# Local attention's first tiles: tables and norms ahead of the last band operations, third rows turned sooner, the output weights' split later

## The reference

```python
x = x + _L0_xattn_ref(_layernorm(x), ctx_1024, ctx_1024, mask)      # band attention, |i - j| <= 128
x = x + _L0_ffn_ref(_layernorm(x), wqkv, ...)                       # two layers of:

h = shift_token(x)                      # second half of the channels from the row before
q, k, v = split(h @ wqkv)               # 8 heads of 64
q = l2norm(q) * q_scale;  k = l2norm(k) * k_scale
q, k = rotary_xpos(q, k)                # q * cos * scale + rotate_half(q) * sin * scale
o = local_attention(q, k, v)            # keys i-256 .. i
x = x + o @ wo
h = layernorm(shift_token(x)) * lg + lb
a, g = split(h @ w1 + b1)
x = x + (a * gelu(g)) @ w2 + b2
```

## Time and profile before

| | us |
|---|---|
| median of 3 runs | 3015.71 (3015.14 to 3015.97) |
| the profiled execution | 3016.03 |
| its span in the profile | 3014.1 |
| PE busy | 2972.0 (99%) |
| DVE / ACT / POOL busy | 1610.6 / 1239.6 / 1135.9 (53%, 41%, 38%) |
| granted PE clock, mean | 0.996 |

### The profile page before, as it was taken

The page is one execution under the profiler, slowest core; times in us unless marked ns, Lnnn a source line. Parts: engine busy times, 40 slices in busy tenths (PEclk is TensorE's granted clock), DMA queues, the critical chain, the costliest instruction groups (busy, mean ns, idle before and its releaser), DMA issues. The chain is left out here.

```text
span 3014.1 us, 44257 instructions
## 1 busy us (share of the span) xinstructions
PE 2972.0 (99%) x17040; PEld 2420.4 (80%) x17040; DVE 1610.6 (53%) x3359; ACT 1239.6 (41%) x2497; POOL 1135.9 (38%) x1200
## 2 busy tenths in 40 slices
PE   8999999999999999999999999999999999999999
PEld 6787888888878888888887788888878888888887
DVE  6975667766765333333324766776675333433331
ACT  6874555555664111111114555555565212111111
POOL 6755556556641101111103555655661111211111
PEclk9999999999999999999999999999999999999999
DMA  7542111111132111001122111111114111111110
GB/s 246 198 162 78 43 39 50 57 43 43 40 104 74 45 45 45 31 20 39 45 78 75 33 43 50 47 50 43 54 57 133 57 45 31 53 55 52 46 53 29
DMA packets 144181, 190.52 MB, mean 63 GB/s; under 512 B 21334, under 2 KB 75098, under 8 KB 143972
## 3 DMA queue, kind: packets, MB, share of 16 engines
q1 hardware_dynamic: 143972, 187.70, 19.6%
HBM read 132.44 MB, written 52.46 MB: 61 GB/s over the span
## 5 line engine op out<-in xcount | busy, mean ns | idle before, releaser
L991 PE MATMUL quad<-fhT_f,w_h_f 128*128 128x512 f32 (+1 forms) x1392 | 551.0, 396 | 1.5 <-ACT w_h_f L1055 1.5
L993 PE MATMUL quad<-fhT_f,w_l_f 128*128 128x512 f32 (+1 forms) x1392 | 545.0, 391 | 0.0
L992 PE MATMUL quad<-fhT_f,w_h_f 128*128 128x512 f32 (+1 forms) x1392 | 543.4, 390 | 0.0
L1650 DVE SCALAR_TENSOR_TENSOR u_f<-quad,bias_f,gate_f_raw 128x512 f32<-128x512 f32 (+1 forms) x174 | 130.4, 750 | 699.0 <-PE quad L993 616.3
L1719 POOL TENSOR_SCALAR stats<-stats 128x1 f32<-128x1 f32 x64 | 43.5, 679 | 1020.2 <-DVE stats L1625 1019.5
L1805 POOL TENSOR_TENSOR turned_qk<-with_cos,with_sin 128x256 f32<-128x256 f32 x256 | 188.8, 759 | 452.4 <-DVE with_cos L1534 361.0
L1210 ACT ACTIVATE lprob<-lprob,small 128x384 f32<-128x384 f32 (+2 forms) x512 | 289.8, 568 | 160.4 <-DVE small L1509 160.4
L1313 ACT ACTIVATE gate_f_raw<-quad,bias_f 128x512 f32<-128x512 f32 (+1 forms) x174 | 119.8, 689 | 506.7 <-PE quad L993 506.7
L1055 ACT ACTIVATE uT_f<-u_f 128x512 fp32r<-128x512 f32 (+2 forms) x176 | 117.5, 668 | 510.9 <-DVE u_f L1650 510.9
L761 PE MATMUL bank_pair<-wqkv_h,hT 128*128 128x512 f32 x992 | 319.8, 403 | 1.1 <-DVE with_sin L1534 1.1
L993 PEld LDWEIGHTS quad<-fhT_f,w_l_f 128*128 128x128 f32 (+1 forms) x1392 | 256.8, 184 | 63.1
(11 more groups left out here) (221 smaller groups left out, 6039.1 us busy)
## 6 DMA issues: line engine op xcount, KB each, us to landing
s_in<-stream SPq DMA_DIRECT2D x128, 128.0 KB, 2.7
s_res<-stream SPq DMA_DIRECT2D x64, 256.0 KB, 2.9
stream<-a_out SPq DMA_DIRECT2D x64, 256.0 KB, 2.0
w_h_f_raw<-in_L_ffn_w SPq DMA_DIRECT2D x60, 256.0 KB, 5.3
h_in_f<-stream SPq DMA_DIRECT2D x112, 128.0 KB, 2.5
res_f<-stream SPq DMA_DIRECT2D x47, 256.0 KB, 3.2
x_in<-in_x SPq DMA_DIRECT2D x32, 256.0 KB, 2.8
ctx_in<-in_ctx SPq DMA_DIRECT2D x32, 256.0 KB, 3.1
```

The lines of the kernel that those rows point to most:

```text
L991: e.matmul(bank[0:n, :], high, hT[:, 0, c, :], start=c == 0, stop=False)
L992: e.matmul(bank[0:n, :], high, hT[:, 1, c, :], start=False, stop=False)
L993: ins = e.matmul(bank[0:n, :], low, hT[:, 0, c, :], start=False, stop=c == KC - 1)
L1650: e.scalar_tensor_tensor(out=Fm.u[q % 2][0:n, :], in0=up_bank(2 * (g * HC + j) + 1)[0:n, :], scalar=Fm.bias1[0:n, 0, j:j + 1], in1=Fm.gate ...
```

## The change

In `band()`, step 36: ACT gets `square(0, 0)`, DVE `norm_sum(0, 0)` ahead of the last `band_add_x`, POOL `scale_tables(0)` and `inverse_norm(0, 0)` ahead of the last `band_offset(.., "x1")`. In `attend` of layer 1, DVE's `norm_sum` of tile 0 stands ahead of its ropes and POOL's `inverse_norm` ahead of its rotation. The key half of tile 0's rotation goes from POOL to DVE (`rotate_first_keys`), with a semaphore of its own. PE turns rows 2 after 12 of tile 1's 24 q and k products, and the order of the turns of q and k and tile 1's v products is new. DVE takes `split_h(s + 1)` ahead of the divisions where the attended tile starts a batch entry. `wo` is split one step later, and an Exp on a small tile is placed in ACT's step 0 of layer 1. Functions that `band()` now calls too move out of `attend`.

```diff
@@ tensor_program, attend
                 if s == 1:
-                    project(l, 1, 12, 36)
+                    project(l, 1, 12, 24)
                     turn_h(2)
+                    project(l, 1, 24, 36)
+                    turn_q(0)
                     project(l, 1, 0, 6)
-                    turn_q(0)
-                    project(l, 1, 6, 9)
                     turn_k(0)
-                    project(l, 1, 9, 12)
+                    project(l, 1, 6, 12)
@@ scalar_program
+        def square(l, t):
...
+                w.wait_ge(S("score_max"), TILES)
+                w.wait_ge(S("total"), BATCH)
+                w.wait_ge(S("key_put"), BATCH)
@@ band
                 if 0 <= s - 6 < TILES:
                     band_put_stream(s - 6)
+                if s == TILES + 4:
+                    square(0, 0)
@@ attend
-                    if d == 0 and rotated_tile(s) is not None:
-                        square(rotated_tile(s))
+                    if d == 0 and rotated_tile(s) is not None and (l or s):
+                        square(l, rotated_tile(s))
...
+                    if l and (s, d) == (0, 0):
+                        e.activation(small[:, 0, 0:16], half_power[:, :], ACT.Exp).then_inc(S("table"), 1)
                     if d == 0 and 1 <= s < TILES - 1:
                         split_h(l, s + 1)
+                    if l and (s, d) == (2, 0):
+                        attend_split_begin(l, 3)
+                    if l and (s, d) == (3, 0):
+                        attend_split_finish(l, 3)
...
-                    if l and (s, d) == (1, 1):
-                        attend_split_begin(l, 3)
-                    if l and (s, d) == (2, 1):
-                        attend_split_finish(l, 3)
@@ vector_program, band
+                if s == TILES + 4:
+                    norm_sum(0, 0)
                 if 0 <= s - 5 < TILES:
                     band_add_x(s - 5)
@@ attend, rope
-                w.wait_ge(S("rotated"), 4 * (n - 1) + 2 * (part + 1))
+                if t or l:
+                    last = (l, t - 1) if t else (l - 1, TILES - 1)
+                    w.wait_ge(S("rotated"), rotated_by_gpsimd(*last, part))
+                if t == 1 and part:
+                    w.wait_ge(S("first_rotated"), 2 * (l + 1))
@@
+            def rotate_first_keys():
+                n, h2 = base, HD // 2
+                turned, cos, sin = (by_head(x[:, 1, :]) for x in (A.turned_qk, A.with_cos, A.with_sin))
+                w.wait_ge(S("with_cos"), 2 * n + 2)
+                w.wait_ge(S("with_sin"), 2 * n + 2)
+                w.wait_ge(S("k_turned"), n)
+                if l:
+                    w.wait_ge(S("f_store", 0), lap(base - GROUP, GROUP))
+                for a, b in ((0, h2), (h2, 0)):
+                    e.tensor_tensor(turned[:, :, a:a + h2], cos[:, :, a:a + h2], sin[:, :, b:b + h2],
+                                    ALU.add).then_inc(S("first_rotated"), 1)
@@
+                    if l and (s, d) == (0, 0):
+                        norm_sum(l, 0)
                     if d == 0 and rotated_tile(s) is not None:
                         rope(rotated_tile(s), 0, A.with_cos, A.rope_cos, "with_cos")
                         rope(rotated_tile(s), 0, A.with_sin, A.rope_sin, "with_sin")
-                        norm_sum(rotated_tile(s))
+                    if d == 0 and rotated_tile(s):
+                        norm_sum(l, rotated_tile(s))
+                    if d == 0 and live and t % TPB == 0:
+                        split_h(s + 1)
...
+                    if (s, d) == (0, 0):
+                        rotate_first_keys()
-                    if d == 0 and 1 <= s < TILES - 1:
+                    if d == 0 and 1 <= s < TILES - 1 and not (live and t % TPB == 0):
                         split_h(s + 1)
+                    for quarter in range(KC):
+                        if l and (s, d) == (2, 1):
+                            attend_split(l, 3, quarter)
...
-                    for quarter in range(KC):
-                        if l and (s, d) == (1 + quarter // 2, 1):
-                            attend_split(l, 3, quarter)
@@ pool_program, band
+                if s == TILES + 4:
+                    scale_tables(0)
+                    inverse_norm(0, 0)
                 if 0 <= s - 5 < TILES:
                     band_offset(s - 5, 4, "x1")
@@ attend
-            scale_tables()
+            if l:
+                scale_tables(l)
             wait_phase()
             for s in range(TILES + 3):
...
+                if l and s == 0:
+                    inverse_norm(l, 0)
                 if rotating is not None:
                     rotate(rotating, 0)
                 if live:
                     divide(t, 1)
+                if rotating:
+                    inverse_norm(l, rotating)
                 if rotating is not None:
-                    inverse_norm(rotating)
                     scale_rotated(rotating, 0)
-                    rotate(rotating, 1)
+                    if rotating:
+                        rotate(rotating, 1)
                     scale_rotated(rotating, 1)
```

More of the change, by code:

```diff
@@ L354, in rotated_tile, with rotated_by_gpsimd @@
         return 0 if s == 0 else s - 1 if 2 <= s <= TILES else None
+    def rotated_by_gpsimd(l, t, part):
+        return 4 * (l * TILES + t) + 2 * (part + 1) - 2 * (l + ((t, part) > (0, 0)))
     def pair_banks(p):
@@ L1149, in split_h @@
             copy(A.hT[n % 2][:, 0, :], rows_bank(l, t)).then_inc(S("hT_high"), 1)
+        def square(l, t):
+            n = l * TILES + t
+            w.wait_ge(S("qk_projected"), n + 1)
+            w.wait_ge(S("norm_sum"), n)
+            if t == 0 and l:
+                w.wait_ge(S("down"), GROUP * GROUPS * HC * l)
+            elif t == 0:
+                w.wait_ge(S("score_max"), TILES)
+                w.wait_ge(S("total"), BATCH)
+                w.wait_ge(S("key_put"), BATCH)
+            i = early_tile(t)
+            if i is not None:
+                w.wait_ge(S("early_store"), 16 * (l * GROUP + i + 1))
+            e.activation(flat(attends[l].square[:, :, :]), flat(qk_banks(t)), ACT.Square).then_inc(S("squared"), 1)
         def band():
@@ L1190, in wait_phase @@
                     w.wait_ge(S("x1"), TILES)
[L1192 to L1203, removed]
             def probabilities(t, h):
@@ L1454, in split_first_rows, with norm_sum @@
             low(h[:, 1, :], rows_bank(l, 0), h[:, 0, :], S("hT_low"))
+        def norm_sum(l, t):
+            n = l * TILES + t
+            w.wait_ge(S("squared"), n + 1)
+            e.tensor_reduce(norm[:, n % 2, 0:16], heads16(attends[l].square[:, :, :]), AX, ALU.add).then_inc(S("norm_sum"), 1)
         def band():
@@ L1521, in split_k @@
                 low(A.kT[:, 1, :, cols], chunks(banks[4]), A.kT[:, 0, :, cols], S("kT_low"))
[L1523 to L1526, removed]
             def rope(t, part, to, table, name):
@@ L1739, in band_masks, with scale_tables, inverse_norm @@
                 e.tensor_scalar(B.key_put[:, :], B.key_mask[:, :], HIDDEN, -HIDDEN, ALU.mult, ALU.add).then_inc(S("key_put"), 1)
+        def scale_tables(l):
+            A = attends[l]
+            w.wait_ge(S("rope_in"), 64 * (l + 1))
+            spread = A.scales[:, :].unsqueeze(1).to_broadcast([P, TPB, 2 * HD])
+            for table in (A.rope_cos, A.rope_sin):
+                e.tensor_tensor(table[:, :, :], table[:, :, :], spread, ALU.mult).then_inc(S("rope_scaled"), 1)
+        def inverse_norm(l, t):
+            n = l * TILES + t
+            nm = norm[:, n % 2, :]
+            w.wait_ge(S("norm_sum"), n + 1)
+            settle(e.tensor_scalar(nm[:, 0:16], nm[:, 0:16], NORM_FLOOR ** 2, 0.0, ALU.max, ALU.add))
+            e.tensor_tensor(nm[:, 16:32], nm[:, 0:16], half_power[:, :], ALU.pow).then_inc(S("norm_inverse"), 1)
         def band():
@@ L1766, in attend @@
             A, base = attends[l], l * TILES
[L1768 to L1772, removed]
             def wait_phase():
@@ L1789, in divide @@
                 e.tensor_scalar(prob, prob, sm[:, 16 + 2 * p:17 + 2 * p], None, ALU.mult).then_inc(S("pscaled_pool"), 1)
[L1791 to L1796, removed]
             def rotate(t, part):
@@ L1811, in scale_rotated @@
                 inverse = norm[:, n % 2, 16 + part * HEADS:16 + (part + 1) * HEADS]
-                w.wait_ge(S("rotated"), 4 * n + 2 * (part + 1))
+                w.wait_ge(S("rotated"), rotated_by_gpsimd(l, t, part))
+                if part and t == 0:
+                    w.wait_ge(S("first_rotated"), 2 * (l + 1))
                 w.wait_ge(S("norm_inverse"), n + 1)
```

## The result

| | before | after |
|---|---|---|
| median, same chip | 3015.37 (3014.78 to 3015.97, 7 runs) | 3023.36 (3022.06 to 3028.49, 7 runs) |
| the profiled execution | 3016.03 | 3023.36 |
| its span | 3014.1 | 3021.6 |
| granted PE clock, mean | 0.996 | 0.998 |

The changed kernel is slower: ratio 1.0029, 95% interval 1.002 to 1.0038. The first tile of layer 0 is sooner, as it should be. Six later tiles lose 12.2 us, which is more than that gain, and layer 1's first tile loses 1.2 us.

What follows compares the result with a forecast made beforehand. PE is busy 99%, so only time it loses or regains counts. First-tile gains of -7.9 and +13.0 for six later tiles give +5.1; slow clock (+7.0, +1.0) makes +13.1: 3029 us, range 3021 to 3037.

Steps and rivals of the forecast that it cites:

- the clock's term: PE at 1.2 GHz behind new gaps: 3.5 us in each layer's first tile, 1.0 for the six other tiles.
- First tile, layer 0: Early norms and PE's new order: first scores at 247.9 instead of 255.46.
- the 0 for the four loads and the last offset: Layer 0's start: last LayerNorm offset and loads come 2.2 us later, cost 0; 2.2 if a load were late.
- First tile, layer 1: Earlier power and keys' rotation off GpSimd: first scores at 1640.6 instead of 1641.72.
- The table load: Layer 1's early Exp moves a 1.28 us load out of tile 0's exponentials; cost 0, at most 1.3.
- The early low part: Tiles 8, 16, 24, both layers: VectorE's wait delays divisions and GpSimd; 1.7, 3.1, 1.7 us each, sum 13.0.
- the 1.1 us for the LayerNorm: Tile 16: early LayerNorm tile follows GpSimd's late divisions, so the keys' low part ends 1.1 us later.
- Tile 0 with the early low part: Later divisions make PE wait 0.3, 2.0 and 2.2 us; tile 1's scores still gain 6.3 and 1.6 us by layer.
- One delay replaces another of the same length: I take 0: Layer 1, moving the split of wo one step later: worth 0, bounds -1.0 and +1.0 us.
- The clock did not hold throughout: Rival, whole run: new gaps too short to lower the clock; sum +5.1, 3020.8 us; chance 0.17.
- nor did it fall in tiles 8, 16 and 24: Rival: clock also falls in these tiles, six times 1.7 us on the forecast; 3038 us; chance 0.13.
- The faster case: Rival, keys' turn of tiles 8, 16, 24: slack swallows VectorE's wait if the shift is below 3.3 us; 3006 us; chance 0.12.

Runs made afterwards that it cites:

- e11: e1 with layer 0's tables, squares, norm sum and power taken behind the band's projection again; 3013.54 us.
- e9: e1 with PE's order of the band's first step put back, third rows turned behind the tile's queries and keys; 3007.66 us.
- e10: e1 with the first tile's key rotation given back from VectorE to GpSimd in both layers; 3006.19 us.
- e1: Changed kernel with VectorE's low part of the turned rows back behind the keys' rope products in every step; 3005.62 us, ratio 0.9967.
- e3: Kernel before with only the early low part, ahead of the divisions where the attended tile starts a batch entry; 3032.89 us, ratio 1.0056.
- e5: Changed kernel with GpSimd's division behind the queries' scaling where the attended tile starts a batch entry; 3006.43 us, ratio 0.997.
- e4: Changed kernel with the four early LayerNorm tiles one step later, so that none meets tile 16; 3021.08 us.
- e7: e1 with the four subtractions of wo moved behind VectorE's low part of the keys, in the same half step; 3004.49 us.
- e6: e1 with the split of wo back in its old place, ScalarE's part at steps 1 and 2; 3007.64 us.
- e2: Changed kernel with the early low part kept at tile 0 alone, undone in tiles 8, 16 and 24; 3011.33 us, ratio 0.9988.

## Why the prediction was right, and where it was off

The direction, the mechanism and its path were right. The forecast was 5.6 us too high: 1.1 of it was gained ahead of layer 0, which no step spoke of, and most of the rest is the clock's term, which was mis-sized.

- **First tile, layer 0.** The first scores, S, were to start at 247.9; with the 1.13 us ahead of layer 0 added back they start at 247.95. e11 shows that the early norms carry it: without them the gap returns. e9 gives PE's new order 0.9 us. The key rotation on VectorE is worth nothing in layer 0 (e10), where GpSimd would have been in time. PE met no wait that would show a late load, so the 0 for the four loads and the last offset held.
- **First tile, layer 1.** S was to be 1640.6. Its row has 1640.94, and 0.28 us of that was lost before layer 1 began (1.4 in the tiles of layer 0, less the 1.1 ahead of them), so it is 1640.66. PE waited 0.19 us for the queries instead of 0.4. e10's marks put the keys' rotation at 0.6 us of it. The table load did move out of tile 0's exponentials, into idle time of ScalarE (1631.53); neither it nor layer 1's new order of norm sum and power was undone by itself, so their shares are not shown.
- **The early low part.** The chain was as forecast at every link: VectorE waits 4.24 us (about 4.2 was asked for), GpSimd's division comes at 422.76 (422.94), the next scores at 433.03 (433.2). e1 and e3 show that nothing else does it, and e5 that GpSimd's order is the path. The six tiles cost 12.2 us where 13.0 was the sum: 1.6 for 1.7, and 2.9 to 3.0 for 3.1. PE's waits were a little shorter (0.25 and 0.46 us for queries and keys, for 0.5 and 0.7), GpSimd's division coming 0.2 us sooner than assumed. In tile 16 the 1.1 us for the LayerNorm measured 1.1 (e4), beside waits that were shorter. The wait for the keys' products is what e5 leaves of each tile's loss: 0.4 us, where 0.5 was put.
- **Tile 0 with the early low part.** The gaps of 2.0 and 2.2 us came as 1.78 and 1.84. In layer 1 the second is 3.05, and there a step failed: "One delay replaces another of the same length: I take 0". The four subtractions were moved to stand beside GpSimd's rotation and scaling, and both engines slowed down (e7): 1.2 us. That the old place cost something too is seen in e6, where the move pays 2.0 us in all. So the term was -2 and not 0 in e1, beyond the bounds of -1.0 and +1.0, and with the subtractions behind the keys, as in e7, it is -3.
- **The clock.** This is the term that was mis-sized: "so I take 3.5 each, +7.0", and 1.0 for the six tiles. Layer 0 fell for 3.4 us and lost 1.5 (changed kernel against e2). Layer 1 fell for 6.8 us: its next scores came at 1660.8 where 1657.4 was forecast without a slow clock; 1.2 of these 3.4 us are GpSimd's slow-down, which leaves some 2.2 for the clock, a difference and not measured alone. An estimate agrees: 2.2 of the 6.8 us lie in PE's wait for the keys (0.62 in 1653.5 to 1656.4) and cost nothing, and half of the other 4.6 is 2.3. The six tiles never fell, in any trace. That makes 3.7 us for the 8.0 I had. The price was taken from the sum of 4.2 us of gaps, by the nearness to the one gap of 4.83. What the rows had for short gaps was the other end, 1.7 us, and three tiles lie there (1.5 in the changed kernel's layer 0, 1.4 in layer 1 of e9 and of e11); where the clock holds it is 0. One execution of the changed kernel is profiled, the one at the median; three of the seven took 3025.0 to 3028.5 us at a mean granted clock of 0.995 or 0.996, so in those the term may have been larger, which no trace shows.
- **The rivals.** The clock did not hold throughout, nor did it fall in tiles 8, 16 and 24. By the rule in the Trainium skill ("TensorE: Matmul & The Clock Gate", section "HAM oscillation — how this bites in real kernels"), a long unbroken idle time takes the clock down. The 4.83 us gap agrees; gaps of 1.8 + 1.8, or one of 1.94 or 1.96 us, took it down too, and others like them did not. The faster case needed a shift below 3.3 us on the keys; GpSimd's division moved by 4.7, so PE's lead took up 3.2 us of it and some 1.6 reached PE. (The terms of that case also add up to 3005.2, not 3006.) e5 reached that case's 3006 us by another way, e1 by leaving the edit out.

What stays open is why the clock falls in one execution and holds in another. e1 and e11 have the same instructions in the same order in layer 1, and no run here tells what decides.

## What to carry to other kernels

Before an instruction that waits is put ahead of others on an in-order engine, find in the trace when its data comes: an instruction that already waits behind 2.4 us of work will wait longer in front of it, and the whole queue with it. Check an edit at each step in which its condition holds: `t % 8 == 0` holds at eight tiles, and the six that are not a layer's first cost 12 of the 17.7 us. Where a wait can't be avoided, look at the next engine's order: one division moved behind the work that PE needs took 1.6 us per tile down to 0.4.

## What the hardware showed that was not expected

- VectorE's subtraction of two SBUF tensors (128x512) takes 0.62 us alone and 1.10 beside GpSimd's additions of two tensors; those take 1.40 us alone and up to 2.29 beside it. GpSimd's two divisions of e1, the first of them beside the same subtractions, took 2.15 us, and 1.20 in e7. The Trainium skill ("GPSIMD Engine Reference", section "1. Specifications") says that the two engines share their SBUF interfaces, with contention where VectorE's instruction has two inputs in SBUF. These rows agree, and give it a price on both sides.
- One order of work with one set of gaps met a clock that fell in one execution and held in another: 1.78 and 1.84 us in the changed kernel against 1.77 and 1.83 in e2; 1.96 in e11 and 1.94 in e9 against 1.93 in e1 and 1.95 in e10. A stretch of 3.4 us at 1.2 GHz behind such a gap cost 1.4 to 1.5 us.
- The 10 us from 21 to 31 us of the band stage ran at 0.50 in some executions (before, e2) and at 1.00 in others (after, e6, e9, e10). Layer 0's first mark moved by 1.1 us between the two traces that were to be compared, and came at 226.83 in e5, where a second stretch, from 55 to 62 us, was slow too.
